# An attention and expert layer on one core: the first batch, the passage between the stages and the end rearranged

## What is computed

```python
x = x + _layernorm(attn(_layernorm(x)))      # x: 16 x 256 x 128
x = x + _layernorm(ffn(_layernorm(x)))
# attn: q, k, v = x@Wq, x@Wk, x@Wv for 16 heads of 64; causal softmax(q k^T / 8) v; heads @ Wo;
#       y = x + that; layernorm(y) * gamma + beta
# ffn:  probs = softmax(x @ router_w); the best 2 of 8 experts of each row;
#       out = sum over the two of prob * (gelu(x @ w1[e]) @ w2[e])    (128 -> 512 -> 128)
```

## Time and profile before

| | |
|---|---|
| median of 3 runs | 734.25 us (733.94 to 735.72) |
| the profiled execution | 735.79 us, of which the span shown is 734.0 us |
| mean granted clock of TensorE | 0.984 |
| TensorE busy | 687.1 us (94% of the span) |
| VectorE busy | 553.2 us (75%) |
| ScalarE busy | 521.7 us (71%) |
| GpSimd busy | 273.2 us (37%) |
| memory read, written | 20.22 MB, 13.56 MB |

### The profile page before, as it was taken

One profiled execution on the slowest core, in us unless ns is written; L12 is line 12 of the kernel. 1 busy time (PEld: TensorE's weight loads), 2 busy tenths in 40 slices (PEclk: granted clock), 3 DMA queues, 4 the chain that ended last, 5 costly groups with the idle time before them and its releaser, 6 DMA issues.

```text
span 734.0 us, 17696 instructions
## 1 busy us (share of the span) xinstructions
PE 687.1 (94%) x5954; PEld 593.1 (81%) x5955; DVE 553.2 (75%) x1914; ACT 521.7 (71%) x1687; POOL 273.2 (37%) x388
## 2 busy tenths in 40 slices
PE   4899999999999999999999999999989999999954
PEld 3688878888888888887888888888868999999921
DVE  5667889888797989888887989898886775444216
ACT  4787777888787877888877878788765664555515
POOL 3022634332323232332323231322322877655535
PEclk9999999999999999999999999999999999999978
DMA  7530000000000000000100000000020234322155
GB/s 182 173 87 8 9 8 12 21 21 18 24 8 23 9 24 8 25 15 16 31 8 23 9 23 8 24 15 10 21 56 24 73 104 132 91 74 84 41 184 174
DMA packets 43701, 34.88 MB, mean 48 GB/s; under 512 B 10624, under 2 KB 40320, under 8 KB 43616
## 3 DMA queue, kind: packets, MB, share of 16 engines
q1 hardware_dynamic: 37984, 23.81, 12.1%
q0 software_dynamic: 4544, 9.45, 3.6%
q10 hardware_dynamic: 1088, 0.54, 0.3%
HBM read 20.22 MB, written 13.56 MB: 46 GB/s over the span
## 4 chain that ended last, share of the span: by engine, by line
PE 65%; ACT 14%; DVE 12%; DMA 3%; issue 3%; POOL 2%; DVEq 1%; SPq 0%; POOLq 0%; ACTq 0%
PE M L684 8%; PE SC L406 8%; PE PT1O L423 8%; PE A L434 5%; PE M L385 4%; ACT prob L1274 4%; PE M L387 4%; PE M L386 4%; PE SC L414 4%; PE SC L409 3%; ACT prob L1268 3%; ACT qk L1263 3%; PE PT1O L442 2%; PE SC L385 2%; PE SC L386 2%
## 5 line engine op out<-in xcount | busy, mean ns | idle before, releaser
L1263 ACT ACTIVATE qk<-M 128x512 f32<-128x512 f32 x127 | 75.9, 598 | 90.0 <-PE M L387 90.0
L1274 ACT ACTIVATE prob<-SC,nmax 128x256 f32<-128x256 f32 x256 | 125.7, 491 | 0.0
L423 PE MATMUL PT1O<-pT,v_sb 128*64 128x256 f32 (+1 forms) x1024 | 98.6, 335 | 0.7 <-ACT pT L1279 0.7
L423 PEld LDWEIGHTS PT1O<-pT,v_sb 128*64 128x64 f32 x1024 | 64.1, 138 | 42.8 <-ACT pT L1279 17.2
L1268 ACT ACTIVATE prob<-SC,nmax 128x128 f32<-128x128 f32 x256 | 95.4, 382 | 3.4 <-DVE nmax L778 3.3
L1544 POOL DMA_INDIRECT expert_rows<-v_sb,got x78 | 77.1, 988 | 46.5 <-ACT v_sb L1418 27.7
L788 DVE TENSOR_TENSOR prob<-prob,rden 128x512 f32<-128x512 f32 x128 | 88.8, 694 | 2.4 <-DVE rden L782 0.2
L1533 POOL DMA_INDIRECT sent_rows<-rec,slot x64 | 66.6, 1040 | 57.7 <-DVE slot L1038 39.3
L778 DVE TENSOR_REDUCE nmax<-SC 128x2 f32<-128x512 f32 x128 | 86.9, 679 | 0.0
L385 PE MATMUL M<-xt_hi,wqk_hi 128*128 128x256 f32 x254 | 82.5, 325 | 3.0 <-DVE xt_lo L772 2.2
L406 PE MATMUL SC<-qk 64*128 64x256 f32 x512 | 84.4, 406 | 0.6 <-ACT prob L1274 0.6
(11 more groups left out here) (186 smaller groups left out, 1777.8 us busy)
## 6 DMA issues: line engine op xcount, KB each, us to landing
got<-sent_rows SPq DMA_DIRECT2D x39, 132.0 KB, 2.3
w_in<-expert_rows SPq DMA_DIRECT2D x16, 256.0 KB, 3.6
x_in<-L_attn_x SPq DMA_DIRECT2D x16, 128.0 KB, 2.2
w_in<-L_ffn_w SPq DMA_DIRECT2D x1, 2048.0 KB, 11.6
x_res<-L_attn_x SPq DMA_DIRECT2D x16, 128.0 KB, 2.1
w_sb<-L_ffn_w SPq DMA_DIRECT2D x8, 256.0 KB, 4.8
out<-y_out SPq DMA_DIRECT2D x8, 256.0 KB, 2.1
sent_rows<-pad_rec SPq DMA_DIRECT2D x11, 132.0 KB, 4.5
```

What stands on the lines that cost most here:

```text
L423: last = mm(PT1O[k * E:(k + 1) * E, cols], v_sb[:, t, h * E:(h + 1) * E], src[:, par, k, :], start=(t == 0), stop=(t == 1), skip_group_che ...
L1263: a.activation(qk[:, p % 2], src[:].rearrange("p (i s) -> p i s", i=2), ACT.Copy).then_inc(qk_sb, 1)
L1274: return a.activation(prob[:, slot, k, 1:3, :].rearrange("p n t -> p (n t)"), SC[par][:, k, LATE_Q], ACT.Exp, bias=nmax[:, par, 0, k:k + 1 ...
```

## The change

- Start: GpSimd's constants behind a wait for wv_ok; wqk_lo of q ahead of the split of x and that of k behind it; 13 and 6 matmuls whose result is not used around the transpose of x; x of batch 1 loaded ahead of wo; x_stats(1), the wait for wo and the cleared tables later.
- Last step and passage: VectorE's and TensorE's order; router pieces 5 and 6 of batch 13 and `finish` of batch 14 into `last_pairs`; the table's last piece one step earlier.
- Places of the last batch: `dispatch` in two parts; one store fewer ahead of the last sends; the pads' row number earlier; `late_table` one half tile later; ACT's pads behind gated(10) and gated(11).
- `back` is laid out so that a partition's eight rows of a group lie together (4 KB).
- The last tile's second product in two banks, gated and stored by halves. Nine matmuls whose result is not used.
- The end in ten parts: the first and the last group in halves. Eight banks for the sums, four slots each for zn and y_out, which lie in other tiles; one load for each part.

```diff
+            pe.wait_ge(sem("mask_ok"), 1)
+            keep_busy(PT0, 13)
             x_transpose(0)
+            keep_busy(PT0, 6)
...
-            qk_low(0)
+            qk_low(0, [0])
             x_split(0)
+            qk_low(0, [1])
...
             inverse_root("x", T, ln_eps, 1)
+            pool.wait_ge(sem("wv_ok"), 1)
             q.memset(ones_bf[:], 1.0)
...
@@ VectorE, step
+                if is_last(b) and u == STEPS - 1:
+
+                    expert_weights(0, w1_at[0])
+                    pT1_copy(p - 1)
+                    maxima(p + 1)
+
+                    dve.wait_ge(sem("gT_mm"), 2)
+                    split_rows(0, 0, M[:, 0:ROWS])
+                    expert_weights(1, w1_at[1])
+                    reciprocals(p)
+                    normalise_pair(p)
+                    return
                 maxima(p + 1)
...
@@ u == 2
+                    if is_last(b):
+                        early_table(5)
+                        w1_at[:] = experts(0, 2)
...
@@ VectorE, last_pairs
-                expert_weights(1, w1_at[1])
+                reciprocals(end - 1)
+                normalise_pair(end - 1, lambda: pT1_copy(end - 2))
                 split_rows(1, 1, M[:, ROWS:2 * ROWS])
-                reciprocals(end - 1)
-                normalise_pair(end - 1)
-                pT1_copy(end - 2)
-                router(B - 2, 0)
+                pT1_copy(end - 1)
+                router(B - 3, 5)
+                finish(B - 2)
                 router(B - 3, 6)
-                pT1_copy(end - 1)
...
@@ first_turn, second_turn
                 if n == 10:
+                    router(B - 1, 6)
+                    send_places(B - 1)
                     late_table(0)
-                    late_table(1)
...
                 if n == 9:
-                    router(B - 1, 6)
                     counts_copy(B - 1, False)
-                    dispatch(B - 1)
+                    find_places(B - 1)
...
@@ GpSimd
-            early_stores(7, 9)
+            early_stores(7, 8)
             send(B - 1)
-            early_stores(9, EARLY)
+            early_stores(8, EARLY)
...
@@ TensorE, the end
+            for _ in range(9):
+                mm(PT0[:], ident[:], wo_sb[:, 0:4].rearrange("p c d -> p (c d)"), start=True, stop=True, skip_group_check=True)
+
+            for n, (g, first, size) in enumerate(PARTS):
+                pe.wait_ge(zz_ld[n], 16)
+                if n >= 8:
+                    pe.wait_ge(sem("zn_done"), n - 7)
                 for r in range(K):
-                    last = mm(sum_bank[g % 4][:], ident[:], zz[:, g % 4, r].rearrange("p t d -> p (t d)"),
+                    last = mm(sum_bank[n % 8][:, 0:size * D], ident[:],
+                              zz[:, g % 4, r, first:first + size].rearrange("p t d -> p (t d)"),
                               start=(r == 0), stop=(r == K - 1))
...
@@ ScalarE, last tile
+            def gated_last(n, k):
+                act.wait_ge(back_st[k], 32 * (n // RING))
+                for t in range(2):
+                    act.wait_ge(sem("out_mm"), n + 1 + t)
+                    a.activation(yo[:, k, t, :], last_banks[t][:, t * D:(t + 1) * D], ACT.Copy,
+                                 scale=got[:, k, t, C_GATE:C_GATE + 1]).then_inc(sem("yo_done"), 1)
```

246 lines of the change are left out of this document (137 added, 109 removed).

## The result

The changed kernel takes **730.65 us** (median of 5 runs, 728.66 to 731.78), the kernel before in the same session 734.05 (5 runs, 733.58 to 735.72). The ratio is 0.9947, with a 95% interval of 0.9927 to 0.9966. It is faster, by 3.4 us and not by the 11.9 of the forecast, and 730.65 lies above the range (718.5 to 727.5).

The account below looks back on a forecast made before the run. TensorE was taken to bound the attention batches, so gains could come only where it waits or clocks low: start 3.8, passage 3.7, places 1.8, end 2.6, together 11.9 off 734.25, giving 722.4 us, range 718.5 to 727.5.

Parts of the forecast that it names:

- Start, 3.8: At the start, xn ready earlier and TensorE kept at work make scores and masks end sooner: 3.8 us.
- Rival 3: At the start, weights' loads and not xn are the pace; only 1 of 3.8 us is left: 725.2, chance 0.05.
- Passage, 3.7: From attention to the expert tiles, a shorter TensorE wait and full clock gain 3.7 us, 0.6 if the clock falls.
- rival 1: In the passage the clock falls all the same, so the gain is 0.6 us: 725.5, chance 0.14.
- I take the gains off the median: Whole kernel: gains from the 735.79 us profiled execution are subtracted from the runs' median of 734.25 us.
- Places, 1.8: TensorE's waits for rows of tile 12 (0.70 us) and tile 16 (1.09) go: 1.8 us for both.
- while the pads gain about 1: Before tile 16, sends begin 1.7 us earlier and pads gain about 1, so the wait falls to about 0.
- End, 2.6: Behind the last tile, the end in ten parts finishes at 731.4 instead of 734.0: 2.6 us.
- The 0.44 of the first store: At the last tile, rows gated in two halves let GpSimd issue the first store 0.44 us earlier.
- the walk: At the end, shifts timed part by part, 2.0 us per whole group; last addition ends at 728.6 instead of 731.22.
- rival 2: The end is paced by transfers or by bridging matmuls and gives 1 us or less: 724.3, chance 0.08.
- Rival 4: Rows stored 4 KB apart slow the tiles' stores, which then set the pace: 744 us at 4.0 per tile, chance 0.03.

Follow-up runs that it names:

- b0: The kernel before, run again without an edit for a second trace, on a chip of the first kind: 733.75 us (one run).
- v3: The changed kernel with its part for the last batch's places undone, on a chip of the first kind: 729.33 us, ratio 0.9943 to the kernel before.
- a0: The changed kernel without an edit, on a chip of the second kind: 767.67 us, ratio 1.009 to the kernel before.
- q3: The kernel before with each loop batch's four sends made in two pairs, on a chip of the first kind: 734.97 us, ratio 1.0014.
- t2: The changed kernel with the eight pads written as pairs of neighbouring rows, on a chip of the second kind: 767.59 us, ratio 1.0094.
- d3: The changed kernel with an unread memset behind GpSimd's last power, on a chip of the second kind: 769.81 us, ratio 1.0114.
- s3: The changed kernel with the old order around the last batch's places, on a chip of the second kind: 763.74 us, ratio 1.0025.

## Why the prediction was wrong

- **Start, 3.8: right.** Measured 3.6 (3.9 beside b0), with xn at 0.60 us and the masks done at 12.0. Rival 3 fell, though a load, that of wv, is now what ScalarE waits for.
- **Passage, 3.7: right beside the trace that it came from, wrong as a gain of the median.** 3.9 us between the two traces; rival 1 fell, with the clock at 1.00 throughout. The step that failed is "I take the gains off the median": the cost of the slow stretch was read from one execution, and most don't have it. The prediction itself says that the profiled execution lay 1.5 us above the median. In b0, with the clock up, the last attention product begins at 556.45, 5.1 us behind the changed kernel's 551.34; 3.9 of that is there since the start (masks at 15.35 and 11.41), so 1.2 is left for the passage. If about a fifth of the runs have the slow stretch, 1.2 + 2.7/5, or some 1.7 us, is what it is worth, an estimate from two traces and the mean clocks: the forecast had 2 us too much. By the Trainium skill (TensorE: Matmul & The Clock Gate, Part 4) transposes don't count as busy the way other matmuls do, and rival 1 took from it that the passage would run at the low clock; the windows show 1.00, with waits of 0.54 to 0.73 us left in it. Other matmuls lie between the transposes, so the rule is not refuted, but the rival is.
- **Places, 1.8: wrong in sign.** The first wait went as forecast (0.7). For the second, the step that failed is that the rows would come earlier by what the sends were issued earlier, "while the pads gain about 1". Beside v3, which has the old order, the last send is issued 1.75 us earlier and the last pad 3.0, and the landing gains 0.5. Nor did the prediction ask what the clock does behind a wait that grows. Measured in the two traces: the lead falls from 7.9 us ahead of tile 16 to 6.7 at it and 5.1 behind it. By v3 the part costs 1.2 us.
- **End, 2.6: nothing.** From the last tile on, the lead went from 5.0 to 4.7 us. The 0.44 of the first store came (5.02 ahead at the last tile, 5.45 at the first load). Of the walk, the step of 2.0 us was right; the step that failed is the first three shifts: it had them 6.1, 8.6 and 10.6 us behind the first load and took the loads as landing in time, where the changed kernel has 7.05, 10.9 and 12.6. That is rival 2, at 0.08, though it allowed for a gain of up to 1 and none came. The last step, 2.8 us from the last addition to the end as before, failed too: it is 3.9, since GpSimd's drain ends some 5 us behind its last power, whatever VectorE does meanwhile.
- Put together, beside b0: 3.9 from the start, 1.2 from the passage, 2.5 lost between the last attention product and the last tile (687.54 in b0, 684.95 in the changed kernel), 0.1 from the end, in all 2.7 (spans 732.0 and 729.3). A fifth of the 2.0 us by which the first trace of before is longer than b0 makes it 3.1, beside 3.4 measured. Of the 2.5 that are lost, the new order has 1.2; v3, with the old one, loses the other 1.3 as well: 0.7 us ahead of tile 9 in both kernels (0.5 of it two new waits of TensorE, at 574.36 and 578.43 in the changed kernel), and most of the rest at tile 16, where v3 waits 1.25 us and b0 0.56. That a lead won ahead of the tiles would partly be lost in them was in no term of the sum. The range left out two terms failing together with the third's size. Rival 4 did not show on the first kind of chip: the last scatters are as far apart as before, and no tile waits for a ring slot.
- On the second kind of chip the change is slower by 0.9% (0.7 to 1.1, a0). No row of the profile that I had showed such holds.

## What to carry to other kernels

Before a gain is taken off the median, ask whether the stretch that it removes is in the median run: a wait with a slow clock behind it is a coin that some executions toss and others don't, and a second profile of the same kernel is worth more than a finer sum. Transfers that are issued earlier need not land as much earlier: here 1.75 and 3.0 us at the issue were 0.5 us at the landing, so ask for the landing of the last of them before counting the gain. And follow each gain to the next wait: TensorE's lead was partly lost among the tiles in either order, and in three traces what was won there turned into idle time before the end's third load, with a slow clock behind it.

## What the runs showed of the hardware

- Behind idle times of TensorE of 2.26, 2.53 (tile 16), 1.89, 2.53 and 2.82 us (end) the next matmuls ran at half speed; behind 1.09, 1.25, 1.31, 1.50, 1.69, 1.74 and 1.79 they did not. Behind 2.15 and 2.16 us in the same place of the same program they once did and once did not, and behind 2.20 (q3) the 8 us from 546 had 0.79. On the second kind of chip they ran slow behind 2.03 (t2), 2.09 (d3) and 2.65 us (s3) at the same place of the end, and not behind 2.25 (a0). So the length of the wait alone does not decide it here.
- GpSimd's last instruction, a drain, ended 5.0 to 5.2 us behind its last operation in every trace, whatever that was (5.1 behind the memset of d3). It is idle time only as long as another engine ends later.
- On three of the five chips of these experiments, semaphore raises of the other engines come up to 11 us late, nearly all in or behind runs of two to fourteen scatters of GpSimd, 0.3 us apart; on the other two, runs as long or longer hold nothing back. That the scatters are the cause is argued from where the late raises lie, not shown.
